# Cross attention on Trainium2: the softmax normalisation's three DMAs moved from SyncE's queue to GpSimd's

## What is computed

```python
q = split(x @ w_q); k = split(text @ w_k); v = split(text @ w_v)      # text: 1593 rows
out_text = merge(softmax(q @ k.T / sqrt(16)) @ v)
out_ip = merge(softmax(q @ (ip @ w_k_ip).T / 4 + mask(boxes)) @ (ip @ w_v_ip))   # ip: 8 rows
out = (out_text + out_ip) @ w_out + b_out + x
```

## Time and profile before

| | us |
|---|---|
| median of 3 runs | 1938.35 (1928.42 to 1939.11) |
| profiled execution | 1930.99 |
| its span, first to last instruction | 1928.6 |
| TensorE busy | 1868.2 (97% of the span) |
| VectorE busy | 1332.4 (69%) |
| ScalarE busy | 1202.6 (62%) |
| GpSimd busy | 305.8 (16%) |
| mean granted clock of TensorE | 0.984 |

### The profile page before, as it was taken

The page is one execution under the profiler, slowest core; times in us unless marked ns, Lnnn a source line. Parts: engine busy times, 40 slices in busy tenths (PEclk is TensorE's granted clock), DMA queues, the critical chain, the costliest instruction groups (busy, mean ns, idle before and its releaser), DMA issues.

```text
span 1928.6 us, 42941 instructions
## 1 busy us (share of the span) xinstructions
PE 1868.2 (97%) x17944; PEld 753.2 (39%) x17944; DVE 1332.4 (69%) x1661; ACT 1202.6 (62%) x2368; POOL 305.8 (16%) x359
## 2 busy tenths in 40 slices
PE   6999999999999999999999999999999999999897
PEld 3333344433444334443344334433344433444332
DVE  5766776677766777677766777667776677676860
ACT  1165666656666666666666666665666656666674
POOL 5112111111111111111111211111112111111000
PEclk9998999999999999999999999999999999999998
DMA  8515434464443633445443543445444363343401
GB/s 235 83 34 135 81 68 90 74 164 72 78 83 69 162 72 72 84 103 134 77 81 68 149 81 68 90 73 162 74 76 88 68 162 70 72 83 69 83 11 45
DMA packets 92035, 175.61 MB, mean 91 GB/s; under 512 B 37473, under 2 KB 60898, under 8 KB 88002
## 3 DMA queue, kind: packets, MB, share of 16 engines
q1 hardware_dynamic: 83426, 141.80, 38.4%
q0 software_dynamic: 5872, 29.11, 4.4%
q10 hardware_dynamic: 2544, 1.97, 0.3%
HBM read 117.75 MB, written 48.82 MB: 86 GB/s over the span
## 4 chain that ended last, share of the span: by engine, by line
PE 85%; DMA 5%; DVE 4%; issue 2%; ACT 1%; ACTq 1%; SPq 1%; POOL 0%; POOLq 0%; DVEq 0%
PE pv_bank L679 23%; PE max_bank L621 20%; PE work_bank L526 11%; PE work_bank L493 10%; PE exp_bank L663 9%; PE work_bank L542 3%; PE work_bank L504 3%; DMA q_stack<-neg_rows 3%; DVE tile_max L950 2%; PE max_bank L632 1%; PE exp_bank L667 1%; PE work_bank L532 1%; ACT probs L846 1%; ACTq L829 1%; DMA scratch_q<-q_parts 1%
## 5 line engine op out<-in xcount | busy, mean ns | idle before, releaser
L846 ACT ACTIVATE probs<-exp_bank 128x512 f32<-128x512 f32 x1920 | 1007.4, 599 | 457.2 <-PE exp_bank L663 445.9
L950 DVE TENSOR_REDUCE tile_max<-max_bank 128x2 f32<-128x1024 f32 x632 | 774.0, 1225 | 436.4 <-PE max_bank L621 432.6
L621 PE MATMUL max_bank<-k_stack,q_stack 48*128 48x512 f32 x1896 | 573.2, 468 | 19.4 <-DVE tile_max L950 17.3
L679 PE MATMUL pv_bank<-probs,v_ones 128*17 128x512 f32 x3840 | 518.5, 603 | 0.0
L952 DVE TENSOR_REDUCE tile_max<-max_bank 128x1 f32<-128x512 f32 x632 | 430.0, 680 | 8.3 <-PE max_bank L621 8.3
L663 PE MATMUL exp_bank<-q_stack,k_stack 50*128 50x512 f32 x1920 | 423.5, 405 | 11.2 <-DMA q_stack<-neg_rows 8.1
L621 PEld LDWEIGHTS max_bank<-k_stack,q_stack 48*128 48x128 f32 x1896 | 236.6, 185 | 416.1 <-issue 267.1
L663 PEld LDWEIGHTS exp_bank<-q_stack,k_stack 50*128 50x128 f32 x1920 | 242.1, 188 | 61.8 <-ACT probs L846 37.8
L493 PE MATMUL work_bank<-ctxt,wk 128*32 128x400 f32 x2496 | 250.8, 507 | 7.4 <-DMA wk<-in_w_k 5.2
L526 PE MATMUL work_bank<-wv,ctxt 128*32 128x320 f32 x3072 | 250.7, 436 | 0.8 <-ACT s_ip L875 0.4
L526 PEld LDWEIGHTS work_bank<-wv,ctxt 128*32 128x32 f32 x3072 | 93.0, 110 | 166.6 <-issue 108.1
(11 more groups left out here) (102 smaller groups left out, 777.1 us busy)
## 6 DMA issues: line engine op xcount, KB each, us to landing
k_stack<-scratch_k SPq DMA_DIRECT2D x240, 200.0 KB, 8.7
scratch_k<-k_parts SPq DMA_DIRECT2D x80, 400.0 KB, 4.8
ctxt<-in_ctx_t POOLq DMA_DIRECT2D x28, 800.0 KB, 8.6
q_stack<-scratch_q SPq DMA_DIRECT2D x240, 64.0 KB, 2.3
scratch_q<-q_parts SPq DMA_DIRECT2D x80, 128.0 KB, 10.1
r_wide<-scratch_r SPq DMA_DIRECT2D x40, 256.0 KB
o_t<-o_sum SPq DMA_DIRECT2D x160, 32.0 KB, 2.0
xres<-in_x SPq DMA_DIRECT2D x8, 640.0 KB, 6.9
```

The costliest lines, as they stand in the source:

```text
L621: nc.tensor.matmul(round_place(n, r)[:, k, :], exact(q_stack[stack, slot, c, t * 128:(t + 1) * 128]), exact(k_stack[stack, slot, c, chunk ...
L679: last = nc.tensor.matmul(pv_bank[h * 32:h * 32 + VW, :], v_ones[:, v_slot(b, kt), head * VW:(head + 1) * VW], p, start=(kt == 0), stop=(k ...
L846: nc.scalar.activation(dst, exp_bank[:, at % BANKS, :], ACT.Exp, scale=SCALE).then_inc(probs_ready, 1)
L950: nc.vector.reduce_max(flat[:, at:at + 2], place[:, 0:2, :], AX.X).then_inc(max_taken, 1)
```

## The change

The three DMAs leave SyncE's program. GpSimd issues them: `load_sums` at the head of a group, before the split of Q; `spread_recips` (`scratch_r`, wait, `r_wide`) before the second split; `scale_o` before the third split in every group, and the table `SCALE_AT` is gone. In group 0 of the first entry there is nothing to normalise. In the last two groups, which have no splits, all of it follows in a row, and after the last group once more. SyncE now begins each group with `load_k` (behind the residual's load in group 0). What is moved, its sizes and its semaphores are the same. The changed kernel's lines have numbers 1 to 14 lower than those of the same lines before.

```diff
-SCALE_AT = (2, 2, 1, 1, 1)
...
-            def normalise(group_no):
-
-                sp.wait_ge(o_read, group_no + 1)
-                sp.dma_start(sums[:, :], o_sum[DH:128:32, :]).then_inc(sums_loaded, 16)
-                sp.wait_ge(recips_ready, group_no + 1)
-                sp.dma_start(scratch_r.rearrange("h (c n) -> (h c) n", n=GH * S // 128), recips[:, :])\
-                  .then_inc(recips_stored, 16)
-                sp.wait_ge(recips_stored, (group_no + 1) * 16)
-                sp.dma_start(r_wide[:, :], scratch_r.unsqueeze(1).to_broadcast([GH, 32, S])).then_inc(r_wide_loaded, 16)
...
-                    if group_no:
-                        normalise(group_no - 1)
                     if group_no + 2 < B * NG:
                         slot_free(group_no + 2)
                         load_k(group_no + 2)
...
-            normalise(B * NG - 1)
             pack(B * NG - 1, NG - 1, None)
...
+            def load_sums(group_no):
+                pool.wait_ge(o_read, group_no + 1)
+                pool.dma_start(sums[:, :], o_sum[DH:128:32, :]).then_inc(sums_loaded, 16)
+
+            def spread_recips(group_no):
+                pool.wait_ge(recips_ready, group_no + 1)
+                pool.dma_start(scratch_r.rearrange("h (c n) -> (h c) n", n=GH * S // 128), recips[:, :]).then_inc(recips_stored, 16)
+                pool.wait_ge(recips_stored, (group_no + 1) * 16)
+                pool.dma_start(r_wide[:, :], scratch_r.unsqueeze(1).to_broadcast([GH, 32, S])).then_inc(r_wide_loaded, 16)
+
             def scale_o(group_no):
...
+                    if group_no:
+                        load_sums(group_no - 1)
                     for n, piece in enumerate(splits):
-                        if n == SCALE_AT[g] and (g or not first):
-                            scale_o(b * NG + g - 1)
+                        if n == 1 and group_no:
+                            spread_recips(group_no - 1)
+                        if n == 2 and group_no:
+                            scale_o(group_no - 1)
...
-                    if len(splits) <= SCALE_AT[g]:
-                        scale_o(b * NG + g - 1)
+                    if len(splits) <= 1:
+                        spread_recips(group_no - 1)
+                    if len(splits) <= 2:
+                        scale_o(group_no - 1)
...
             batches(body)
+            load_sums(B * NG - 1)
+            spread_recips(B * NG - 1)
             scale_o(B * NG - 1)
```

More of the change, by code:

```diff
@@ L1167, in body @@
                 for g in range(NG):
+                    group_no = b * NG + g
                     splits = [p for p in SPLITS[g] if not (last and p[1] > 4)]
+                    if group_no:
+                        load_sums(group_no - 1)
                     for n, piece in enumerate(splits):
-                        if n == SCALE_AT[g] and (g or not first):
-                            scale_o(b * NG + g - 1)
+                        if n == 1 and group_no:
+                            spread_recips(group_no - 1)
+                        if n == 2 and group_no:
+                            scale_o(group_no - 1)
                         if piece[0] == "K":
```

## The result

The changed kernel takes **1954.89 us** (median of 6 runs, 1947.31 to 1966.72). The kernel before, in 6 runs of its own, took 1932.57 us (1926.68 to 1939.11). The ratio is 1.0118, with a 95% interval of 1.0083 to 1.0153: slower by 1.2%, 22 us, where 1929 us and "within 1%" had been forecast, and a small gain.

A forecast was written before the change was run, and what follows sets the result against it. TensorE, busy 97% of the span, was taken to set the time. From the profiled 1930.99 us, -9.4 + 2 + 3 gave 1926.6 us; the median was put at 1929 us, range 1911 to 1972.

The forecast's parts named there:

- All seven waits of L663: TensorE's waits for the maximum's two small transfers, 8.1 us in all, were to go with the context's load 7 us earlier.
- the term of +2: Last normalisation: three DMAs in a row from GpSimd's queue take 2 us more than the 8.7 before; bounds -3 and +6.
- The sentence on the longest of the seven waits: Behind TensorE's longest wait for the maximum's transfers (2.57 us), the clock at 0.73 over 5 us costs 1.35 us more.
- the slow clock around 180 us: Slow-clock stretch at 180 to 200 us, around the first of the seven waits: 4.4 us more if it goes too.
- term one: Group 1 of every entry: earlier context's load removes the seven waits and a clock loss, -9.4 us; bounds 0 and -13.8.
- alone worth nothing: K stack's load 13 us earlier, Q stack's about as much: no gain by itself, as TensorE shows no wait for stacks.
- the term for the sums: VectorE's reciprocal at visit 2 waits for sums beside the K stack's load: +3 us, 0.4 in each of eight groups 2.
- the first rival: Sums land only after the K stack's load and Q's store: 43 us over some 36 groups, 1967 us; chance 0.18.
- the sums come late in every group: The title of the first rival: slower, up to 2016 us if the clock falls behind each stop.
- its point of decision: The first rival holds from a landing of the sums 5.6 us behind issue in group 2, 6.7 in group 1.
- the rival's 1967: Time in us if the first rival holds without the clock's share: 1926.6 - 3 + 43.

The follow-up runs named there:

- e1: The changed kernel with the sums' transfer back on SyncE's queue ahead of the K stack's load: 1916.01 us, 0.9902 of the kernel before.
- e3: The changed kernel with VectorE's reciprocal at visit 4 in place of 2: 1917.06 us, 0.9899 of the kernel before.
- e2: The changed kernel with SyncE waiting for the sums to land before issuing the K stack's load: 1918.08 us, 0.9925 of the kernel before.
- e8b: The changed kernel with the reciprocal at visit 4 and the very last group's three transfers on SyncE's queue: 1912.03 us, 0.9893 of the kernel before.
- e6: The changed kernel with the sums issued by ScalarE right behind its copy: 1940.7 us, 1.0019 of the kernel before.
- e4: The kernel before with GpSimd issuing the context's load without waiting for a stack: 1934.66 us, 0.9997 of the kernel before.
- e7: The changed kernel with group 2's load of x moved behind the scaling: 1949.57 us, 1.0068 of the kernel before.
- e5: The changed kernel with SyncE holding the store of Q until the sums have landed: 1952.53 us, 1.0091 of the kernel before.

## Why the prediction was wrong

**What came as forecast.** SyncE issues the K stack 4.4 to 5.6 us before ScalarE's copy ends ("about 5 us"). The context's load of group 21 leaves 20.0 us behind the copy, where it was 29.3, with no wait in brackets. All seven waits of L663 are gone. The last normalisation takes 10.6 us from the copy ("10 to 11"), so the term of +2 was +1.9. One reading behind that term was off: the packets of the load issued at 1089.31 begin at 1090.58, 1.27 us behind the issue and not "up to 1 us", and the sums' first packet on idle DMA engines is 1.2 to 1.4 us behind its issue on either queue. The sentence on the longest of the seven waits holds to the tenth: 2.57 + 1.35 = 3.9 us were to be had there, and that group became 3.96 us shorter. And the part given as a bound only, the slow clock around 180 us, goes for the greater part too. Before the change it began ahead of the window that the prediction read; windows of the kernel before, then of e1:

```profile
160.00:180.00 20.00, 18.42 (x104) 7.56 (x101) 13.92 (x19) 11.90 (x24) 5.87 (x9) 0.79 0.55 171
```

```profile
160.00:180.00 20.00, 18.36 (x132) 7.68 (x128) 15.84 (x23) 12.85 (x26) 5.79 (x9) 0.91 0.67 215
180.00:200.00 20.00, 18.53 (x186) 7.48 (x190) 15.78 (x21) 12.76 (x25) 3.86 (x6) 1.00 0.65 110
```

The clock is 0.91 and 1.00 there in place of 0.79 and 0.78, and the group around it 6.0 us shorter. So term one, -9.4 with -13.8 as its end, was -15.8 us in e1 and -18.0 in e3, where nothing else stands against it, and -12.5 in the changed kernel. Two parts stand in it. In the later entries e1, e2, e3 and e8b all gain 9.8 to 9.9 us in groups 1, near the 8.5 us of the -9.4 that lay there (the first entry's wait was 0.9 us). In the first entry they gain 3.9 to 8.1 us, with the clock at 0.89 to 1.00 in these two windows, and e6, whose clock is 0.81 and 0.85 there, gains 2.6. That part differs from kernel to kernel, and one profiled execution of each doesn't say how much of it is chance. So the forecast term was near, and its bound was too small: 160 to 180 us had been left out of it. e4 adds what the account left out: the context's earlier load alone is worth nothing, since the Q stack would then be late. The prediction had called the stacks' earlier loads "alone worth nothing"; so is the context's, and both together are the gain.

**The step that failed** is the term for the sums, "I take +3". It is mis-sized more than ten times, 35 us for 3: groups 0, 2, 3 and 4 lost 1.4 + 22.3 + 3.9 + 4.6 = 32 us, and groups 1 gained 3.3 us less than in e1, 35 us in all. Its mechanism was right, and the prediction had said where to look; what was wrong are its two inputs.

The first is when the small transfer lands. I had the K stack's load end 10.3 us behind its issue, from the one load that ran alone, which gave 5.2 us for the sums. Measured from the issue of the K stack to the reciprocal: 10.9 to 13.5 us, 12.3 in group 17. The trace also holds each packet with its queue, size and time, and so the 96 pieces of 12.8 KB of a K stack's load. In group 17 the load was issued 4.66 us ahead of the sums where 5.1 had been read, its last piece ended 11.3 us behind its issue and not 10.3, and the reciprocal came 1.0 us behind that piece: 5.2 + 0.4 + 1.0 + 1.0 = 7.7 us. Over all 37 groups the last piece ends 9.9 to 11.5 us behind the issue of the load, median 10.6, and the reciprocal stands 0.8 to 2.9 us behind that piece, median 1.4. The windows of group 21 of the changed kernel, with the sums issued at 1067.43 and the reciprocal at 1074.63:

```profile
1066.00:1070.00 4.00, 4.00 (x54) 1.81 (x50) 2.52 (x4) 3.10 (x7) 2.05 (x3) 1.00 1.05 139
1070.00:1074.00 4.00, 4.00 (x39) 1.39 (x32) 1.82 (x2) 2.22 (x5) 0.00 (x0) 1.00 0.78 119
1074.00:1075.00 1.00, 1.00 (x14) 0.37 (x16) 0.37 (x2) 1.00 (x3) 0.00 (x0) 1.00 0.04 13
```

The column before the last, the share, is what I should have read. The DMA engines are full (1.05) at only 139 GB/s. My argument against the first rival was that this load moves 119 GB/s where the context's moved 326, "so it leaves more room beside it". GB/s is no measure of room; the share is. In the kernel before, windows over the lone K stack's load and over the context's load (there with SyncE's transfers beside it) say the same:

```profile
80.00:84.00 4.00, 3.08 (x46) 1.07 (x34) 1.60 (x5) 0.70 (x2) 0.00 (x0) 1.00 1.00 128
...
1095.00:1100.00 5.00, 4.88 (x51) 2.52 (x43) 3.51 (x7) 2.77 (x7) 0.00 (x0) 1.00 1.01 414
```

Both fill the engines, at 128 and at 414 GB/s. The row was at hand before the prediction. A piece of the K stack's load holds a DMA engine for 1.6 us on the median, one of the context's (6.4 KB) for 0.24.

The second input is what else is in the way. I gave group 2 alone 0.4 us for its output stores. They are not in the way: in group 17 their issues end at 875.91, the last score's end (L653, 877.11) lets the load go at 877.15, and in groups 1, which have no such stores ahead, the load leaves the same 4.7 us before the sums. But in groups 2 VectorE wants the sums 4.4 us behind their issue, elsewhere 4.9 to 5.5, and x comes behind (e7). So in group 17 VectorE was 3.25 us late where 0.6 had been worked out, and 3.2 on the mean of the eight.

**The rivals.** It went the way of "the sums come late in every group". They do, in all 37, and its point of decision (5.6 us behind the issue in group 2, 6.7 in group 1) was passed in nearly all. Of its details one fell: the store of Q, which made its landing late in my working, does nothing (e5). Its price per group was near: 1.2 us forecast, 35 / 37 = 0.9 measured. With term one at -15.8 and not -9.4, 35 us and not 43 for the sums, and without the clock's loss behind each stop, of which these traces show little, that comes to 23 us (-15.8 + 35, and 1.9 at either end); the medians differ by 22, and the rival's 1967 stood for 36. It had a chance of 0.18 against 0.48, and the argument that kept it down was the one on GB/s.

**The rule and the row.** The Trainium skill, DMA: Bandwidth & Descriptors, "Queues, rings and completion order", has each DMA engine take its queues in turn, a packet at a time, from which the prediction took that a small transfer on a queue of its own should come through early. The runs speak against that: 7.1 us on GpSimd's queue and 6.7 on ScalarE's, beside 2.1 to 2.3 alone. The same section also says that a transfer's completion is an ordered write that lands behind every earlier write of that DMA engine, on whichever queue. By that alone the data could be early and only the completion late. The packets take the two apart. Queues of the changed kernel from the issue of the sums in group 21 (1067.43) to 1071.80, then from there to the reciprocal (packets, MB, share of the 16 engines; q1 is SyncE's queue, q0 GpSimd's):

```profile
q1 hardware_dynamic: 87, 0.56, 97.8%
```

```profile
q1 hardware_dynamic: 305, 0.28, 52.1%
q0 software_dynamic: 32, 0.01, 4.3%
```

For 4.4 us none of the sums' packets ran, though on idle DMA engines the first one comes 1.3 us behind the issue; over the 37 groups it came 3.2 to 5.1 us behind it. In group 17 the 16 packets that carry the sums start, one by one and within 0.03 us, where the last 16 pieces of the K stack's load end. So it is the data that waits, until the load's pieces are through, and not the completion alone. It isn't so for every pair of queues: in the kernel before, over 1095 to 1100 us, the context's load and SyncE's transfers had packets side by side:

```profile
q0 software_dynamic: 243, 1.35, 65.7%
q1 hardware_dynamic: 241, 0.72, 35.6%
```

So queues do take turns there, and beside the six pieces of a K stack's load that each DMA engine has they didn't. Why, no run here shows.

## What to carry to other kernels

Before a bulk load goes ahead of a small transfer, look for the in-order engine that waits for the small one: here 8 KB took 7 us in place of 2, and VectorE's maxima and then TensorE stood behind it. Judge the room beside a load by the share of the DMA engines, not by GB/s: 128 GB/s left no more of it than 414 did. If the wait can't be kept clear of the load, move the consumer a little later (one number, `INVERT_AT`, turned 1.2% slower into 1.0% faster), or let only the small transfer go first, which was all that the kernel before did right.

## What the hardware showed that I hadn't expected

- A K stack's load (six DMAs of 200 KB into 16 partitions each) fills the DMA engines at 128 to 139 GB/s, in pieces of 12.8 KB that take 1.6 us each on the median; the context's load and SyncE's transfers beside it fill them at 414.
- An 8 KB transfer beside it lands when it drains, on GpSimd's queue as on ScalarE's, and whether it writes SBUF or DRAM: `sums` 5.6 to 8.8 us in place of 2.3, `scratch_r` outside groups 2 a median 7.6 us (e1) and 8.8 us (e2) from its issue to the issue of `r_wide`, in place of 2.0 in the last group. In group 17 of the changed kernel the packets of `sums` start where the last pieces of the load end.
- From GpSimd's queue on idle DMA engines the chain of three transfers took 10.3 us, from SyncE's 8.5 to 8.7: 0.5 to 0.6 us for each.
- TensorE's granted clock fell to half for a part of the last group in three of ten profiled executions (after, e4, e5), which cost 8 to 13 us, and in the other seven it did not. The changed kernel and e7 have the same last group, and it took 12.7 us longer in the one and nothing in the other. That is more than some of the terms in question, so one profiled execution's span is not to be read without its windows.
